# A third buffer for token rows, one store counter for each batch, and expert slots taken ahead of two shared-expert pieces

## The reference

```
logits = x @ gate_w.T
scores = softmax(logits)                       # 64 experts
topk_w, topk_i = top_k(scores, 6)
# tokens of each expert, in order of their number; the first CAP = 32 are kept
y   = (silu(buf @ w_gate) * (buf @ w_up)) @ w_down      # buf: 64 experts x 32 tokens
out = sum over the kept slots of a token of topk_w * y
shared = (silu(x @ sw_gate) * (x @ sw_up)) @ sw_down
x = layernorm(x + out + shared)
```

## Time and profile before

| | us |
|---|---|
| median of 3 runs | 1562.5 |
| lowest and highest | 1559.62, 1572.12 |
| the profiled execution | 1566.63 |
| span of its trace | 1564.9 |
| TensorE busy | 1428.3 (91%) |
| VectorE busy | 947.1 (61%) |
| ScalarE busy | 573.6 (37%) |
| GpSimd busy | 556.2 (36%) |

### The profile page before, as it was taken

The page is one execution under the profiler, slowest core; times in us unless marked ns, Lnnn a source line. Parts: engine busy times, 40 slices in busy tenths (PEclk is TensorE's granted clock), DMA queues, the critical chain, the costliest instruction groups (busy, mean ns, idle before and its releaser), DMA issues.

```text
span 1564.9 us, 23981 instructions
## 1 busy us (share of the span) xinstructions
PE 1428.3 (91%) x8106; PEld 1133.3 (72%) x8106; DVE 947.1 (61%) x2170; ACT 573.6 (37%) x1441; POOL 556.2 (36%) x483
## 2 busy tenths in 40 slices
PE   7899999999999999889999799999999999766990
PEld 6677777777777777666776578888788788653660
DVE  4577777777777777744343356647566565655214
ACT  4344444444444444622121134333343333321330
POOL 2755555555555555001012213423513522203223
PEclk9999999999999999999899899999999999879996
DMA  5000000000011000010000020020110002944994
GB/s 171 8 4 8 5 10 0 10 0 10 0 42 27 0 0 13 8 61 0 1 0 0 0 73 9 8 75 8 29 53 10 10 8 59 265 150 145 288 260 121
DMA packets 68218, 76.35 MB, mean 49 GB/s; under 512 B 14205, under 2 KB 55445, under 8 KB 68149
## 3 DMA queue, kind: packets, MB, share of 16 engines
q1 hardware_dynamic: 56789, 58.49, 13.2%
q10 hardware_dynamic: 8288, 12.22, 2.6%
q0 software_dynamic: 3072, 4.72, 1.6%
HBM read 66.22 MB, written 9.21 MB: 48 GB/s over the span
## 4 chain that ended last, share of the span: by engine, by line
PE 76%; DVE 11%; POOL 4%; issue 4%; ACT 3%; DMA 2%; another core or an unknown queue 1%; DVEq 0%; ACTq 0%; POOLq 0%
PE ps L1610 37%; PE ps L1726 8%; PE ps L1711 6%; PE ps L1699 4%; PE ps L1846 4%; PE ps L1756 4%; PE ps L1704 2%; PE ps L2052 2%; DVE acc L1164 2%; PE ps L1923 1%; DVE prod L1054 1%; PE ps L2117 1%; PE ps L1913 1%; DMA sums_dram<-rows 1%; PE ps L2134 1%
## 5 line engine op out<-in xcount | busy, mean ns | idle before, releaser
L614 POOL TENSOR_TENSOR qk<-q,ksb 128x512 f32<-128x512 f32 x64 | 82.6, 1290 | 303.9 <-ACT q L838 213.8
L753 ACT ACTIVATE probs<-ps,nm 128x128 f32<-128x128 f32 (+3 forms) x256 | 133.8, 525 | 144.9 <-DVE nm L1114 144.9
L1726 PE MATMUL ps<-kT,qT 128*128 128x128 f32 (+3 forms) x512 | 175.5, 452 | 7.3 <-ACT probs L753 7.3
L1037 DVE TENSOR_TENSOR pT_low<-ps,pT 128x384 fp32r<-128x384 f32 (+2 forms) x256 | 100.2, 449 | 103.4 <-ACT pT L696 97.9
L1054 DVE TENSOR_TENSOR prod<-ps,rope_sb 128x1024 f32<-128x1024 f32 x128 | 150.0, 1213 | 13.7 <-PE ps L1610 11.3
L696 ACT ACTIVATE pT<-ps 128x384 fp32r<-128x384 f32 (+2 forms) x256 | 86.5, 415 | 160.2 <-PE ps L1756 160.2
L492 POOL TENSOR_TENSOR qT<-prod 64x512 f32<-64x512 f32 x64 | 83.5, 1305 | 172.2 <-DVE prod L1054 169.7
L1711 PE MATMUL ps<-U,oT 128*128 (+1 forms) x512 | 124.6, 386 | 0.7 <-ACT oT L696 0.7
L1114 DVE TENSOR_REDUCE nm<-ps 128x1 f32<-128x128 f32 (+3 forms) x256 | 114.6, 483 | 11.5 <-PE ps L1728 11.5
L492 POOL TENSOR_TENSOR kT<-prod 64x512 f32<-64x512 f32 x64 | 82.1, 1282 | 106.3 <-DVE prod L1054 103.7
L1164 DVE SCALAR_TENSOR_TENSOR acc<-ps,rinv,acc 128x256 f32<-128x256 f32 x256 | 108.8, 478 | 15.9 <-PE ps L1711 15.9
(11 more groups left out here) (256 smaller groups left out, 2754.8 us busy)
## 6 DMA issues: line engine op xcount, KB each, us to landing
eg<-in_L_ffn_w_gate_dram SPq DMA_DIRECT2D x16, 704.0 KB
eg<-in_L_ffn_w_up_dram SPq DMA_DIRECT2D x16, 704.0 KB
ed<-in_L_ffn_w_down_dram ACTq DMA_DIRECT2D x10, 640.0 KB
ksb<-ks_dram SPq DMA_DIRECT2D x16, 256.0 KB, 3.3
ed<-in_L_ffn_w_down_dram SPq DMA_DIRECT2D x6, 640.0 KB
rows_dram<-rows ACTq DMA_DIRECT2D x4, 640.0 KB, 3.3
acc<-in_L_attn_x_dram SPq DMA_DIRECT2D x4, 512.0 KB
wq_in<-in_L_attn_wq_dram SPq DMA_DIRECT2D x8, 256.0 KB, 2.8
```

Source lines behind the costliest of these rows:

```text
L614: nc.gpsimd.tensor_tensor(qk[:], q3[:], ksb[b % 2][:], ALU.mult).then_inc(qk_ready, 1)
L753: nc.scalar.activation(probs[hh][:, off:off + (i + 1) * P], ps[:, BS + i % 2, 0:(i + 1) * P], ACT.Exp, bias=nm[:, hh, i:i + 1], accum_out= ...
L1037: return nc.vector.tensor_tensor(o, whole, hi.bitcast(F32), ALU.subtract)
L1726: pe.matmul(ps[:, bank, 0:(i + 1) * P], qT[:, hh, b, i * P:(i + 1) * P], kT[:, hh, b, 0:(i + 1) * P], start=True, stop=False)
```

## The change

There are three row buffers; the third lies at 85 KB, where the weights of expert group 5 are loaded later. Each batch has a counter of its own for its stores: the first the old semaphore, the others three semaphores that earlier parts of the program have finished with, from the count at which those left them (`rows_stored_first`). `wait_rows(engine, b)` waits for all the stores of batch b. It stands in `rows4(3)` for batch 0, in SyncE's stream for batch 2 ahead of the load of group 5, and in GpSimd's ahead of the gathers for all four. `rows4(2)` and `store_rows` wait for no store. In VectorE's order `take_slots()` comes right behind `merge_lists()`, ahead of `hidden4(1, 1)` and `hidden4(1, 2)`.

```diff
--- before.py
+++ after.py
@@ -182,7 +182,7 @@
         sw = [place(f"sw{h}", 20 + 5.5 * h, [P, KD, 2, F1S], F32R) for h in range(2)]
         gwT = [place(f"gwT{h}", 31 + 0.5 * h, [P, KD, E1], F32R) for h in range(2)]
         x3T = [[place(f"x3T{i}{h}", 32 + 8 * i + 4 * h, [P, KD, T], F32R) for h in range(2)] for i in range(3)]
-        rows = [place(f"rows{i}", 56 + 5 * i, [P, TPB, ROW]) for i in range(2)]
+        rows = [place(f"rows{i}", at, [P, TPB, ROW]) for i, at in enumerate((56, 61, 85))]
         e4 = place("e4", 66, [P, TPB, E1])
         marked = place("marked", 67, [P, 2, 2, E1])
         lists = place("lists", 68, [P, BATCH * CAP])
@@ -254,8 +254,7 @@
         gw_turned, consts4 = sem("gw_turned"), sem("consts4")
         x3_ready, x3_turned, x3hi_ready, x3lo_ready = sem("x3_ready"), sem("x3_turned"), sem("x3hi_ready"), sem("x3lo_ready")
         logits4, nmx4_ready, exp4, scored = sem("logits4"), sem("nmx4_ready"), sem("exp4"), sem("scored")
-        rows_stored, gate4_ready, gated4_ready, hid4_ready = (
-            sem("rows_stored"), sem("gate4_ready"), sem("gated4_ready"), sem("hid4_ready"))
+        gate4_ready, gated4_ready, hid4_ready = sem("gate4_ready"), sem("gated4_ready"), sem("hid4_ready")
         marked_ready, marked_turned, kept_ready, slots_turned = (
             sem("marked_ready"), sem("marked_turned"), sem("kept_ready"), sem("slots_turned"))
         down4, shared_done = sem("down4"), sem("shared_done")
@@ -290,6 +289,8 @@
         gu_loaded, lb_loaded, la_loaded, dn_loaded = sem("gu_loaded"), sem("lb_loaded"), sem("la_loaded"), sem("dn_loaded")
         e_loaded = x_in + [gu_loaded, lb_loaded]
         e_loaded_first = (16, 16, 16, 16, 32, 64)
+        rows_stored = [sem("rows_stored"), rope_loaded, la_loaded, dn_loaded]
+        rows_stored_first = (0, 16, 16 * 8, 16 * 13)
         w0_hi, w0_lo = sem("w0_hi"), sem("w0_lo")
         dchain = sem("dchain")
         var_ready, rstd_ready = sem("var_ready"), sem("rstd_ready")
@@ -317,6 +318,10 @@
             return 7 if h else 4 if b < 2 else 2
 
         down_dram = io["L1_ffn_w_down"].rearrange("x (p k) n -> p x (k n)", k=2)
+
+        def wait_rows(engine, b):
+
+            engine.wait_ge(rows_stored[b], rows_stored_first[b] + (48 if b == 0 else 32))
 
         def wait_gathered(engine, quarters):
 
@@ -450,6 +455,7 @@
             for s in (3, 4):
                 load_experts(s)
             sp.wait_ge(sw_lo, 2)
+            wait_rows(sp, 2)
             load_experts(5)
             for s in range(RING, GROUPS):
                 sp.wait_ge(gu4_ready, s - RING + 1)
@@ -673,7 +679,8 @@
             nc.gpsimd.iota(lane[:], pattern=[[P, 2]], base=TOK, channel_multiplier=1,
                            allow_small_or_imprecise_dtypes=True).then_inc(consts4, 1)
             pool.wait_ge(idx_ready, 2)
-            pool.wait_ge(rows_stored, 32 * BATCH + 16)
+            for b in range(BATCH):
+                wait_rows(pool, b)
 
             for s in range(GROUPS):
                 nc.gpsimd.indirect_dma_start(out=xg[:, s, :], out_offset=None, in_=rows_dram,
@@ -931,15 +938,13 @@
 
             def store_rows(b):
                 act.wait_ge(scored, b + 1)
-                if b:
-                    act.wait_ge(rows_stored, 32 * b + 16)
-                here = rows[b % 2]
-                nc.scalar.dma_start(rows_dram[b * T:(b + 1) * T, :].rearrange("(i p) n -> p i n", p=P), here[:]).then_inc(rows_stored, 16)
+                here = rows[b % 3]
+                nc.scalar.dma_start(rows_dram[b * T:(b + 1) * T, :].rearrange("(i p) n -> p i n", p=P), here[:]).then_inc(rows_stored[b], 16)
                 nc.scalar.dma_start(sums_dram[b * T:(b + 1) * T, :].rearrange("(i p) n -> p i n", p=P),
-                                    here[:, :, 0:D]).then_inc(rows_stored, 16)
+                                    here[:, :, 0:D]).then_inc(rows_stored[b], 16)
                 if b == 0:
                     nc.scalar.dma_start(sums_dram[TOK:TOK + 2 * P, :].rearrange("(i p) n -> p i n", p=P),
-                                        here[:, 0:2, 0:D]).then_inc(rows_stored, 16)
+                                        here[:, 0:2, 0:D]).then_inc(rows_stored[b], 16)
 
             def gate4(b, m):
                 f, size = F1T[m]
@@ -1406,12 +1411,12 @@
             def rows4(b):
 
                 dve.wait_ge(rstd_ready, b + 9)
-                if b >= 2:
-
-                    dve.wait_ge(rows_stored, 32 * (b - 1) + 16)
+                if b >= 3:
+
+                    wait_rows(dve, b - 3)
                 for i in range(TPB):
                     t = b * TPB + i
-                    nc.vector.tensor_scalar(rows[b % 2][:, i, 0:D], acc[:, t, :], meanvar16[:, t, 0:1], rstd16[:, t:t + 1],
+                    nc.vector.tensor_scalar(rows[b % 3][:, i, 0:D], acc[:, t, :], meanvar16[:, t, 0:1], rstd16[:, t:t + 1],
                                             ALU.subtract, ALU.mult).then_inc(x3_ready, 1)
 
             def x3_rests(b):
@@ -1458,7 +1463,7 @@
                 link(nc.vector.reciprocal(sm4[:], sm4[:]))
                 settle()
                 link(nc.vector.memset(top4[:, :, TOP1:8], -1.0))
-                nc.vector.tensor_tensor(rows[b % 2][:, :, D:ROW], e4[:], bcast(sm4[:].rearrange("p (i a) -> p i a", a=1), [P, TPB, E1]),
+                nc.vector.tensor_tensor(rows[b % 3][:, :, D:ROW], e4[:], bcast(sm4[:].rearrange("p (i a) -> p i a", a=1), [P, TPB, E1]),
                                         ALU.mult).then_inc(scored, 1)
                 settle()
                 for i in range(TPB):
@@ -1502,9 +1507,9 @@
             list_tokens(3)
             hidden4(1, 0)
             merge_lists()
+            take_slots()
             hidden4(1, 1)
             hidden4(1, 2)
-            take_slots()
 
             def match_slots(q):
                 dve.wait_ge(idx_turned, q + 1)
@@ -2002,7 +2007,7 @@
                 wait_past(pe, x3lo_ready, b * KD)
                 for k in range(KD):
                     for i in range(TPB):
-                        last = pe.transpose(ps[:, k, i * P:(i + 1) * P], rows[b % 2][:, i, k * P:(k + 1) * P], ident[:])
+                        last = pe.transpose(ps[:, k, i * P:(i + 1) * P], rows[b % 3][:, i, k * P:(k + 1) * P], ident[:])
                     last.then_inc(x3_turned, 1)
 
             def logits(b):
```

## The result

| | before | changed |
|---|---|---|
| median | 1566.89 us | 1557.88 us |
| lowest and highest | 1559.62, 1572.74 | 1552.0, 1562.23 |
| runs | 12 | 12 |
| profiled execution | 1566.63 | 1552.0 |
| span of its trace | 1564.9 | 1550.3 |

The ratio is 0.9936 (95%: 0.9919 to 0.9953), 0.64% faster, which is 10.0 us of 1566.9; the two medians lie 9.0 us apart. The forecast was 10.9 us and 1551.6 us, range 1542 to 1558: a change within 1%, as given with a chance of 0.84. The time itself, 1557.88 us, lies 6.3 us above the forecast and only 0.1 us inside the range. Of these 6.3 us, 4.4 come from the base: the median before was 1562.5 us over 3 runs and is 1566.9 over 12.

The account below looks back on a forecast made before the run. TensorE, busy for 91% of the 1564.9 us span, was taken as the bound. Gains of 10.2 us (stall and clock) and 0.7 us (slots) make 10.9, so 1562.5 becomes 1551.6 us, range 1542 to 1558.

Parts of the forecast that it names:

- The stall: Routing stage, rows4(2): VectorE idle 8.58 us for a store of batch 0's rows; the third buffer removes 8.6 us.
- the clock behind it: Transposes and gate_up4(0, 2) after rows4(2): TensorE keeps its full clock, 0.86 + 0.73 = 1.6 us more.
- The sum's smaller term: The 1.6 us from TensorE's kept clock, within the 10.2 us by which list_tokens(1) starts earlier.
- The waits that were costed at nothing: rows4(3) on batch 0's stores, group 5's later load, and the gathers' waits on stores and counters: zero cost each.
- slower than before: Rival: group 5's load ahead of batch 3's stores holds the gathers; 1571.3 us with twice 15.3 us; chance 0.04.
- The clock in the next batch: Rival: TensorE's clock also stays up at down4_products(0, 0), 2.7 us more, 1548.9 us; chance 0.13.
- Slots ahead: take_slots before two hidden pieces: gathers start 1.5 us earlier, rows_of(0) 0.7 us earlier, between 0.3 and 1.5.
- the wait behind `gate_up(0)`: 8.22 us wait for an unexplained signal beside the gathers; length left unchanged. Rival: undone, 1543.5 us; chance 0.1.
- the prediction's own last sign: Last condition for being wrong: the wait after gate_up(0) has another length.
- its end is tied to the last gather: Rival on the wait after gate_up(0): slots gain 1.5 in place of 0.7 us, 1550.8 us; no separate chance.
- The sum: Whole kernel: 10.2 + 0.7 = 10.9 us gained, 1551.6 us against the median of 1562.5.
- All of it moves as one: Expert loop, scatters and last norm: nothing behind the change gives back the 10.9 us.

Follow-up runs that it names:

- buffers only: Changed kernel with take_slots() back in its old place behind the two hidden pieces; third buffer and counters kept: 1557.83 us, ratio 0.9928.
- slots only: Kernel before, two row buffers and one counter, with take_slots() right behind merge_lists(): 1570.22 us, ratio 1.0009.
- changed again: The changed kernel run once more, nothing altered, in another session: 1559.35 us, ratio 0.9957.
- filled and piece: Changed kernel with gate_up4(2, 0) and gate_up4(2, 1) right behind gate_up(0), and hidden4(0, 1) ahead of list_tokens(1): 1563.25 us, ratio 0.9974.
- gate_up after gathers: Changed kernel with TensorE waiting for all 16 gathers before gate_up(0): 1561.11 us, ratio 0.9952.
- piece before list: Changed kernel with hidden4(0, 1) ahead of list_tokens(1) on VectorE: 1552.86 us, ratio 0.9925.
- filled: Changed kernel with two shared-expert pieces, gate_up4(2, 0) and gate_up4(2, 1), right behind gate_up(0): 1549.58 us, ratio 0.9917.
- gathers paused: Changed kernel with GpSimd stopping after eight of the sixteen gathers until gate_up(0) is done: 1555.13 us, ratio 0.9915.
- buffers again: Changed kernel with take_slots() in its old place, run once more in another session: 1556.20 us, ratio 0.9935.
- buffers, paused: Changed kernel with take_slots() in its old place and GpSimd's last eight gathers behind gate_up(0): 1555.22 us, ratio 0.9914.
- filled, slots last: Changed kernel with gate_up4(2, 0), gate_up4(2, 1) behind gate_up(0), hidden4(0, 1) ahead of list_tokens(1), take_slots() in its old place: 1559.55 us, ratio 0.9950.

## Why the prediction was right, and where it was not

**The stall** (8.58 us) and the clock behind it (1.6 us): right. Forecast 10.2 us at `list_tokens(1)`, measured 10.5 in the changed kernel and 10.4 with the buffers alone, or 10.2 in both when the 0.2 to 0.3 us that lie ahead of `list_tokens(0)` are taken off. The sum's smaller term shows in VectorE's idle time ahead of it, 0.97 us where 2.33 - 1.6 = 0.73 was expected. At the end of the run buffers alone are worth 9.0 to 9.2 us of stretch, and 9.7 and 10.9 us between medians.

**The waits that were costed at nothing**: right. `rows4(3)` starts at 37.06 (forecast 37.2, from 1383.2) with no idle time put down to a store. The load of group 5 is issued here (SyncE):

```profile
1386.29 0.38 SPq L437 DMA_DIRECT2D eg<-in_L_ffn_w_gate_dram  x1
```

that is at 48.05 of the stage, forecast 48.5. It meets the stores of batch 3 as argued, the last of which is issued at 1391.38; in the changed kernel's windows all that traffic ends some 3 us ahead of the first gather at 1401.48:

```profile
1398.00:1399.00 1.00, 1.00 (x6) 0.81 (x5) 0.92 (x4) 0.00 (x0) 0.00 (x0) 1.00 0.36 127
1399.00:1400.00 1.00, 0.73 (x4) 0.24 (x2) 0.90 (x4) 0.00 (x0) 0.00 (x0) 1.00 0.01 2
```

The gathers start 0.30 us behind the end of `gidx`, as before, with three more waits on their path. The slowest of the whole-batch stores into `sums_dram` (L943) landed after 8.3 us (13.9 before). The traffic that the rival "slower than before" feared was there, but it was over before the gathers wanted to start, so it cost nothing.

**The clock in the next batch** did not stay. In all 14 profiled executions `down4_products(0, 0)` took 5.4 to 5.5 us, behind 3.3 us of idle time or 2.5. The rule of the Trainium skill quoted with that rival ("TensorE: Matmul & The Clock Gate", Part 1: the looks run freely) would have left it to luck; at this place no trace shows any luck. In the loop of the attention layer the same code had 0.90 in one execution and 1.00 in another, which agrees with it.

**Slots ahead** is the term that failed, with its sign. Forecast +0.7 us, between 0.3 and 1.5. Its working holds up to the point where it stopped: gathers 1.3 to 1.9 us earlier for this edit alone (forecast 1.5), and `rows_of(0)` 1.0 us earlier (71.16 for 72.19 with the buffers alone; forecast 0.7). But `gate_up(0)` behind it is already 0.6 us later (74.15 for 73.57). The step that fell is the treatment of the wait behind `gate_up(0)`: "Since it lies beside the gathers it should move with them, and I leave its length." It moves with them, but its length doesn't stay. With slots ahead and no pause its end stands 3.5 to 3.8 us behind the issue of the last gather (changed, slots only, changed again, filled and piece), and it begins on the first transposes; with slots last it comes in two or three pieces, the first of them over before the last gather is issued. The hold is 11.9 us long in place of 8.7 before and 4.7 to 7.1 with the buffers alone, and the stretch is 2.0 to 2.2 us longer with the buffers and 3.6 to 3.7 in the other two pairs (before and slots only, the two filled ones). By the prediction's own last sign ("if the wait after gate_up(0) has another length") it was wrong here. Of the rivals named for it one had "its end is tied to the last gather", at +1.5 us in place of +0.7: the right tie for the slots-ahead kernels, but priced as if the hold of before had that tie too. There it ends before the last gather is issued (92.59 for 94.37).

**The sum**: 10.2 + 0.7 = 10.9 was forecast. In the stretch it was 9.0 to 9.2 for the buffers less 2.0 to 2.2 for the slots, 6.8 to 7.2; set against set 7.3 and 7.8; between the medians 9.0; by the ratio 10.0. That the last two come so near the forecast is in part the mix of executions, which is luck. So is that 1557.88 us lies in the range at all: its upper end allowed the median of before to be 2 us off, and it was 4.4.

**"All of it moves as one"** holds only in part. From "taken" to the end it is 126.0 to 126.3 us in before, changed, slots only and gate_up after gathers (125.5 in changed again), 130.4 to 131.7 in piece before list, filled and gathers paused, and 129.2 to 131.6 in the three that have the buffers without the slots (buffers only, buffers again, buffers, paused). So of the 11.8 us by which "piece before list" takes the result of `gate_up(0)` earlier than the changed kernel, 6.2 reach the end. Where the others go can be read in its TensorE rows, at two later `gate_up`s, of which these are the longer wait and a window behind it:

```profile
1492.38 1.39 PE L2122 MATMUL ps<-eg,xsT 128*32 128x352 f32 x16 [3.38 <-issue]
```

```profile
1495.00:1500.00 5.00, 5.00 (x21) 3.33 (x14) 0.00 (x0) 0.00 (x0) 0.00 (x0) 0.50 1.07 375
```

Together they wait 4.7 us with the DMA engines full (share 1.09 to 1.12 from 1480 to 1495), and the clock falls behind the second. "Filled" has one such wait of 4.7 us, and the changed kernel, in the same stretch, none over 0.5. That fits weights that have not landed yet when the loop runs earlier; no run took the loads away to show it.

**What stays open**: what the hold is. Shown is that it moves to where gathers are in flight (gathers paused, gate_up after gathers), that the signal itself is late and not its reader, and that work on TensorE doesn't end it (filled and piece). That it isn't fixed by the code is likely but not shown by a profile: two kernels had none in one session, the changed one and their sum had it in another, on one chip, but no kernel was profiled in both. What speaks for it is the kernel before, which ran in both: its median was 1562.4 us in the session without the hold (11 runs) and 1567.1 in the other (35 runs), and with only the runs whose mean clock lies below 0.965 it is 1562.4 and 1568.3. Why that session had none was not found. It bears on the verdict: what this change is worth where nothing is held was not measured.

## What to carry to other kernels

A buffer that removes a wait for a store is worth the idle time and the clock that the idle time cost, and both can be read off TensorE's and VectorE's rows. An edit that brings DMAs forward has to be costed against the work that now runs beside them: here 1.3 to 1.9 us on the gathers cost 2 to 3.7 us. When two profiled executions are compared, first subtract what differs ahead of the change.

## What the runs showed of the hardware

- While GpSimd issued indirect gathers (16, each 128 rows of 1280 bytes, one every 1.25 us), results of TensorE were taken up to 10.5 us after their matmuls were over (changed kernel, ends near 1413.8, taken 1424.26), with no releaser in the trace. ScalarE and SyncE, which both wait for that signal, went on within 0.01 us of each other (1424.26 and 1424.25), so the signal was late. Matmuls issued during that time ran at full pace in one kernel (24 in 5.91 us, "filled and piece") and one by one, with pauses of 0.95 to 1.65 us, in another (1428.14 to 1434.81, "filled, slots last"). In one session on a chip that showed it in another, it was absent from three kernels.
- TensorE went from 2.4 to 1.2 GHz (granted clock 1.00 to 0.50) at the same place in every profile, `down4_products(0, 0)` (5.41 to 5.49 us for 2.76), in a pause of 3.3 us without a matmul, and in three kernels of 2.5; in one of 0.71 us (changed kernel, 1365.11) it did not.
- Unchanged code ahead of the change came out 6 to 9 us apart between executions (first `rows4` at 1338.2 to 1338.8 us in 4 profiles, at 1344.7 to 1347.3 in 10), with granted clocks between 0.90 and 1.00 in the same window of the attention layer.
